# A graph-network kernel's target stages: gathers issued behind TensorE's first subtraction of five gathers back, with five row buffers

## What is computed

```python
def _gnn_layer(nf, traj, src, dst, We, be, Wn, bn):
    ef = jnp.concatenate([nf[src], nf[dst], traj[:, None]], axis=-1)
    msg = jax.nn.leaky_relu(ef @ We.T + be, negative_slope=0.01)
    red = jax.ops.segment_sum(msg, dst, num_segments=nf.shape[0])
    h = jnp.concatenate([nf, red], axis=-1)
    return jax.nn.leaky_relu(h @ Wn.T + bn, negative_slope=0.01)
...
x = _layernorm(x + _L0_gnn_ref(x, L0_gnn_Wh, L0_gnn_weight, src, dst), axis=-1)
x = _layernorm(x + _L1_gnn_ref(x, edge_weight, src, dst, ...), axis=-1)
```

## Time and profile before

| what | us |
|---|---|
| median of three runs | 10442.16 |
| lowest and highest run | 10429.43, 10443.02 |
| span of the profiled execution | 10466.8 |
| the three target stages, from first gather to last sum, in that span | 5274 to 6522, 7190 to 8443, 9111 to 10367 |

### The profile page before, as it was taken

The page is one execution under the profiler, slowest core; times in us unless marked ns, Lnnn a source line. Parts: engine busy times, 40 slices in busy tenths (PEclk is TensorE's granted clock), DMA queues, the critical chain, the costliest instruction groups (busy, mean ns, idle before and its releaser), DMA issues. The chain is left out here.

```text
span 10466.8 us, 546251 instructions
## 1 busy us (share of the span) xinstructions
PE 8877.0 (85%) x200294; PEld 7617.9 (73%) x200294; DVE 8717.3 (83%) x16671; ACT 7435.1 (71%) x19555; POOL 4345.7 (42%) x4286
## 2 busy tenths in 40 slices
PE   7999999546997666659988888999888989989987
PEld 6999999324775555558877777787777768877775
DVE  6999999456998999978878787787887878778877
ACT  7888887003666999966777777677777767677776
POOL 0000000455002777734455555345555534455553
PEclk9999999656999999969999999999999999999998
DMA  1000000023666888849988888698788859978875
GB/s 44 8 10 8 8 8 6 19 42 101 210 209 203 253 253 254 248 115 290 294 256 248 248 249 215 208 293 273 248 248 248 243 160 293 295 247 249 249 247 150
DMA packets 1298246, 1948.78 MB, mean 186 GB/s; under 512 B 192607, under 2 KB 831081, under 8 KB 1297257
## 3 DMA queue, kind: packets, MB, share of 16 engines
q1 hardware_dynamic: 1052054, 1285.20, 36.7%
q0 software_dynamic: 245248, 650.66, 24.2%
q10 hardware_dynamic: 304, 4.93, 0.1%
HBM read 1225.54 MB, written 719.25 MB: 186 GB/s over the span
## 5 line engine op out<-in xcount | busy, mean ns | idle before, releaser
L1832 POOL DMA_INDIRECT work<-rows,oct_at x1752 | 2148.6, 1226 | 1609.9 <-DVE work L1957 1448.1
L1663 PEld LDWEIGHTS bank<-work 128*128 128x128 fp8e4 (+1 forms) x56064 | 1938.1, 98 | 477.3 <-issue 289.5
L1663 PE MATMUL bank<-work 128*128 128x64 bf16 x56064 | 2107.4, 193 | 110.8 <-issue 87.7
L1957 DVE TENSOR_TENSOR work<-bank,work 128x512 f32<-128x512 f32 x1752 | 1206.8, 689 | 768.1 <-PE bank L1908 616.1
L1908 PE MATMUL bank<-work 128*128 128x64 bf16 x42048 | 1600.5, 193 | 186.8 <-issue 138.5
L1607 PE MATMUL bank<-work 128*128 128x64 bf16 x34560 | 1567.4, 193 | 5.7 <-issue 5.7
L1908 PEld LDWEIGHTS bank<-work 128*128 128x128 fp8e4 x42048 | 1391.5, 98 | 214.4 <-issue 171.8
L1607 PEld LDWEIGHTS bank<-work 128*128 128x128 fp8e4 x34560 | 1412.4, 98 | 174.5 <-issue 9.7
L1858 ACT CAST work<-bank 128x512 bf16<-128x512 f32 x1752 | 1026.4, 586 | 542.6 <-issue 374.2
L1626 DVE TENSOR_SCALAR work<-bank,part 128x512 fp8e4<-128x512 f32 x1440 | 1029.0, 750 | 283.0 <-PE bank L1587 282.6
L1961 DVE SCALAR_TENSOR_TENSOR bank<-work 128x512 f32<-128x512 f32 x1752 | 1216.9, 695 | 4.5
(11 more groups left out here) (363 smaller groups left out, 20361.0 us busy)
## 6 DMA issues: line engine op xcount, KB each, us to landing
work<-hits_g SPq DMA_DIRECT2D x1752, 256.0 KB
rows<-work SPq DMA_DIRECT2D x1440, 256.0 KB
hits_g<-work SPq DMA_DIRECT2D x584, 256.0 KB
rows<-work SPq DMA_DIRECT2D x480, 260.0 KB
work<-hits_s SPq DMA_DIRECT2D x720, 128.0 KB, 3.1
work<-rows,oct_at POOLq DMA_INDIRECT x2336
hits_s<-work SPq DMA_DIRECT2D x240, 128.0 KB
side<-meta POOLq DMA_DIRECT2D x720, 20.0 KB, 3.1
```

The lines of the kernel that those rows point to most:

```text
L1663: last = ten.matmul(to[:, 0:D], hits_of(j), piece_of(j), start=j == 0 and k == 0, stop=j == OCT - 1 and k == 2, skip_group_check=True)
L1832: pool.indirect_dma_start(octs[g % ROWS], None, table_octs, bass.IndirectOffsetOnAxis(ap=oct_at[:, g:g + 1], axis=0)).then_inc(s_octs[g % ...
L1957: vec.tensor_tensor(total[g % 2], z[g % BANKS][:, :], octs[g % ROWS], ALU.add).then_inc(s_added, 1)
```

## The change

Two numbers and one wait change. The row buffers of the three target stages become five, which makes the region `work` 308 columns larger. And POOL's wait ahead of gather g is no longer for VectorE's addition of group g-4 (`s_added`), but for TensorE's first subtraction of group g-5 (`s_less`). As that subtraction needs the high piece, which needs the leaky ReLU, which needs the addition, the buffer of group g-5 has been read by then. The gathers of a stage, their sizes and their order stay the same.

```diff
-WORK = 13900
+WORK = 14208
...
     def target_phase(number, stored, ready, table):
...
-        HITS, ROWS, WINDOWS, BANKS, MIDS, LOWS = 12, 4, 4, 6, 6, 4
+        HITS, ROWS, WINDOWS, BANKS, MIDS, LOWS = 12, 5, 4, 6, 6, 4
...
         @block.gpsimd
         def _(pool):
             for g in range(NG):
-                at_least(pool, s_added, g - ROWS + 1, since)
+                at_least(pool, s_less, g - ROWS + 1, since)
                 pool.indirect_dma_start(octs[g % ROWS], None, table_octs,
                                         bass.IndirectOffsetOnAxis(ap=oct_at[:, g:g + 1], axis=0)).then_inc(s_octs[g % GATHERED], 16)
```

## The result

The changed kernel took 10361.33 us (median of four runs, 10358.64 to 10363.56) beside 10442.59 us before: a ratio of 0.9922, 95% interval 0.9908 to 0.9936. That is 81 us less. Every ratio in this document is of the runs that the record counts as fast; one was not, a run of 10579.06 us among f2's nine. The prediction said 10222 us, 220 us less: the right side, within the stated range, and almost three times the gain. Later runs showed more than that: in some sets of runs the kernel before takes 9735 us, and there the same change makes it slower.

What follows compares the result with a forecast made beforehand. It took TensorE's completions, held until about 1.5 us after a gather's start, as the bound. (2.113 - 1.97) x (1752 - 210) = 220 us off the 10442.2 us median gave 10222 us; range 10080 to 10445.

Steps and rivals of the forecast that it cites:

- What bounds the kernel: Target stages: POOL's gathers hold back TensorE's matmul completions until about 1.5 us after their start; 2.113 us a group.
- The fifth buffer at nothing: Row buffers at each target stage's start: gain bounded by nothing and 1 us a stage, taken as nothing.
- The lead as covered: Gather's start to its own addition: 5.42 us against a 4 us landing, 1.4 us slack, cover gone at 6.9 us.
- The loop: Target-stage cycle: release, subtraction's completion 0.03 or 0.22 us, 0.27 until POOL starts, 1.49 to 1.6 until the hold ends.
- between the two forms: Target-stage group time taken as 1.97 us, since branches and register loads break the rhythm now and then.
- the fast form: Target-stage loop at 1.79 to 1.90 us a group; as a rival throughout, 1.86 us, 390 us less, 10052, chance 0.04.
- slow form: Target-stage loop at up to 2.09 us a group; as a rival everywhere, 35 us gain, 10407, chance 0.11.
- second rival: Target stages: hold falls on `scatter` and `before_message`, TensorE stalls; 2.2 to 2.3 us a group, 10576, chance 0.13.
- my first: Rival, target stages: each gather starts 0.49 us after TensorE's result; 2.09 us a group, 35 us gain, 10407, chance 0.11.
- 0.22 if it was not: Target-stage loop: time until the first subtraction's completion is out, 0.22 us if not held, 0.03 us if held.
- The tail of each stage: Last 70 or so gathers of each target stage, 2.16 us a group: no change expected, left out of the gain.
- a rival at 0.10: Target stages: hold not of the gather's making, or its cost moves elsewhere; 2.113 us a group stays, 10442, chance 0.10.

Runs made afterwards that it cites:

- f2: Changed kernel with six row buffers and gather g waiting for `before_message` of g-3; prompt set: 9771.7 us, 1.0032 of the kernel before.
- h2: Changed kernel with six row buffers and gather g waiting for `before_message` of g-3; held set: 10193.59 us, 0.976 of the kernel before.
- i1: Changed kernel with five buffers kept, but POOL waiting for VectorE's addition of g-5; held set: 10520.35 us, 0.9991 of the kernel before.
- i2: Changed kernel with POOL's indirect gather replaced by a plain load of the same bytes; held set: 9869.86 us, 0.9374 of the kernel before.
- i3: Changed kernel without POOL's target-stage gathers, SP loading rows into four buffers; held set: 10519.69 us, 0.9992 of the kernel before.
- i4: Changed kernel with gather g waiting for VectorE's leaky ReLU of g-4, five buffers; held set: 10955.81 us, 1.0404 of the kernel before.
- g1: The changed kernel unaltered, run again; prompt set: 9795.77 us, 1.0064 of the kernel before.
- k2: Changed kernel with a sixth row buffer, gather g waiting for the first subtraction of g-6; prompt set: 9729.31 us, 1.0 of the kernel before.
- f1: Changed kernel with five buffers kept, but POOL waiting for VectorE's addition of g-5; prompt set: 9732.57 us, 0.9997 of the kernel before.
- k1: Changed kernel with seven row buffers, four middle-piece buffers, gathers behind `before_message` of g-4; prompt set: 9734.3 us, 1.0003 of the kernel before.
- j1: Changed kernel with seven row buffers, four middle-piece buffers, gathers behind `before_message` of g-4; held set: 10194.98 us, 0.9763 of the kernel before.
- f4: Changed kernel without POOL's target-stage gathers, SP loading rows into four buffers; prompt set: 10347.82 us, 1.0623 of the kernel before.
- g: A prompt set of runs, with nothing changed by the label itself; the kernel before took 9734.97 us in it.
- j: A held set of runs, with nothing changed by the label itself; the kernel before took 10444.75 us in it.

## Why the prediction was right in sign and wrong in size

**What bounds the kernel** was read rightly. Rows 4 to 6 side by side pointed to held completions, and h2, i1, i2, i3 and i4 bear it out: a group of the same size takes 1.77, 1.95, 2.06, 2.1 or 2.4 us a group by what POOL issues and when. The last is 900/376 of i4.

**The fifth buffer at nothing**: right (0.9997 and 0.9991).

**The lead as covered**: right in the sets like the first result, since six buffers changed nothing there (0.9924 and 0.9915 against 0.9922 and 0.9919). It was a matter of the group's time, though. The prediction named 6.9 us of landing as the point where the cover ends. That sum was wrong: it adds the slack of 1.4 us, which is the lead of 5.42 less a landing of 4, to the lead itself and so counts it twice. An addition would start late from a landing of 5.42 us on. At 1.8 us a group the cover had ended with a lead of about 4.9 us (g1, k2).

**The loop** is the step that failed. The prediction put the group "between the two forms" at 1.97 us and said that TensorE's own step of 1.73 us would carry it to the fast form. The profile shows 2.059 us, near the slow form's 2.09. With it the sum gives (2.113 - 2.059) x 1542 = 83 us, and 81 came. TensorE does not get ahead: what it could have gained in a round, it loses inside the next `before_message` (1.14 us for 0.86 in the timeline, over 1.0 us in 1089 of 1410 groups). That it stalls there because the hold also falls on `scatter` is my reading. What the runs show is that the long `before_message` comes with indirect gathers in a held set, and in none of the 1410 groups of f1, g1, k1 or k2 (prompt sets) or of i2 (plain loads). That stall is the mechanism of my second rival, at the size of my first: I had priced it at 2.2 to 2.3 us a group and not seen that after it the addition follows at once (0.04 us). The remedy was in the same sum: the term "0.22 if it was not" belongs to the subtraction, and a gather behind `before_message` drops it (h2, 0.976, which is nearly what I had forecast for the change).

**The tail of each stage**, which I left out of the gain, did gain a little: the last 70 groups of the three stages took 2.15, 2.22 and 2.17 us each and take 2.14, 2.17 and 2.09 now, about 9 us together. With it the working comes to 92 us. In the two traces the three stages (first to last matmul of `scatter`) are 87 us shorter and the spans 104, 15 of these ahead of the first of them. So the closeness of 83 to the 81 between the medians is partly luck.

**The pages of the Trainium skill.** "PE and ACT never wait on anyone" ("SBUF — State Buffer", "Who interferes with whom") was weighed as a rival at 0.10. No run here bears it out in a held set: with an indirect gather under way TensorE waits, with a plain load it does not (i2). In the prompt sets the trace agrees with it (0.04 us in f1).

## What to carry to other kernels

Where a consumer starts late although its producer's record has ended, set the late starts against what other engines issue at that time, not only against the semaphore that ended the wait. A DMA's place in the order has two prices, the lead to its consumer and what its issue does to others: buffers buy the first, the choice of the event it waits for sets the second, and they can be tuned apart (j1, k1). And a gain of under 1% that hangs on such a coincidence should be timed on several occasions before it is kept.

## What the runs showed of the hardware that I had not expected

- In some sets of runs the results of TensorE's matmuls reach VectorE late while POOL issues an indirect DMA (181 of 181 cases, until 1.44 us after the gather's start in the median), and TensorE's own matmuls are drawn out; in others neither happens (0 of 705 in f1). The hold of completions is the reading that fits both. The target stages of the kernel with five buffers took 1249 to 1253 us (`scatter`'s first to last matmul, i1) and 1052 to 1055 us (f1). The part ahead of the first layer's target stage also differs, 3323 against 3131 us. These 192 us arise where POOL issues other indirect DMAs (lines 1053 and 1211, 354 in all, from 1949 us on): the hundredth vector instruction of line 1441 behind them starts at 2593.5 us in i1 and 2401.9 in f1, and the last of its 960 at 3287.4 and 3095.0, the same distance later, with no POOL work from 2600 to 3200 us in i1. Not every stage with gathers differs: the first layer's own (584 at line 1695) takes 1219 us in both i3 and f4. Both kinds were seen on chips of one number (g and j), so it is not settled what sets it.
- A plain DMA of the same bytes on the same queue shows no hold (i2: 1.77 us a group in a held set).
- A gather keeps POOL 1217 to 1250 ns when it starts behind VectorE's addition (before, f1, i1) and 956 to 977 ns behind TensorE's results or behind the leaky ReLU (after, f2, i4). Behind the addition it starts while the leaky ReLU runs, which reads `total` twice. Within one run too the length goes by that: in h2 the 87 gathers that start during the leaky ReLU take 1203 ns in the median, the 1568 that start during the addition 958. The Trainium skill, "SBUF — State Buffer", section "Who interferes with whom", says that a VectorE instruction with two SBUF inputs contends with a GpSimd instruction that reads SBUF, and that the one issued first decides who waits. The durations fit that; no run changed it alone. It cost the kernel nothing that the times show.
